# Two transformer layers with a mixture of experts: attention scores from two rounded 32-bit parts, even and odd heads on the two row halves of TensorE

## The reference

```
# layer 0: pre-norm
x = x + attn(ln1(x), ln1(x), causal)          # call 0
x = x + attn(ln2(x), context)                 # call 1
x = x + relu(ln3(x) @ w1 + b1) @ w2 + b2      # FFN, 256 -> 1024 -> 256
# layer 1: post-norm, all norms with gain and shift
x = ln1(x + attn(x, x, causal))               # call 2
x = ln2(x + attn(x, context))                 # call 3
top-2 of 8 experts by softmax(x @ router), shares = softmax of the two weights
x = ln3(x + sum of share * (gelu(x @ e_w1 + e_b1) @ e_w2 + e_b2))
# attn: 16 heads of width 16, softmax(q k^T / 4) v, then an output projection
```

## Time and profile before

| | |
|---|---|
| median of 3 runs | 1273.6 us (1271.52 to 1281.05) |
| the profiled execution | 1274.6 us |
| its span in the trace | 1272.8 us |
| PE busy | 1107.4 us (87%) |
| DVE busy | 836.6 us (66%) |
| ACT busy | 685.6 us (54%) |
| POOL busy | 561.3 us (44%) |

### The profile page before, as it was taken

The page is one execution under the profiler, slowest core; times in us unless marked ns, Lnnn a source line. Parts: engine busy times, 40 slices in busy tenths (PEclk is TensorE's granted clock), DMA queues, the critical chain, the costliest instruction groups (busy, mean ns, idle before and its releaser), DMA issues. The chain is left out here.

```text
span 1272.8 us, 26559 instructions
## 1 busy us (share of the span) xinstructions
PE 1107.4 (87%) x9056; PEld 911.7 (72%) x9056; DVE 836.6 (66%) x1782; ACT 685.6 (54%) x1445; POOL 561.3 (44%) x805
## 2 busy tenths in 40 slices
PE   8789999999999999999999998877289999989840
PEld 7567677778877888877777666544289998989840
DVE  2666667775555444355676777642479999999945
ACT  4355555665555554445566655644176666656522
POOL 4355555322221113345674554433436565656544
PEclk9899999999999999999999989977589999999985
DMA  7666657573333233446575754405477676767663
GB/s 162 99 134 125 95 81 97 85 126 59 51 49 49 39 36 51 84 59 93 119 104 74 106 91 81 77 26 184 148 231 221 195 226 195 236 192 223 208 159 114
DMA packets 106707, 152.20 MB, mean 120 GB/s; under 512 B 19440, under 2 KB 91376, under 8 KB 99824
## 3 DMA queue, kind: packets, MB, share of 16 engines
q1 hardware_dynamic: 98112, 140.09, 50.5%
q0 software_dynamic: 8352, 10.80, 4.4%
q10 hardware_dynamic: 144, 0.02, 0.0%
HBM read 78.39 MB, written 21.62 MB: 79 GB/s over the span
## 5 line engine op out<-in xcount | busy, mean ns | idle before, releaser
L862 ACT ACTIVATE probs<-s 128x384 f32<-128x384 f32 (+1 forms) x512 | 267.8, 541 | 195.2 <-PE s L680 181.8
L932 DVE TENSOR_REDUCE neg_max<-s 128x2 f32<-128x512 f32 x256 | 169.6, 689 | 95.4 <-PE s L657 89.2
L930 DVE TENSOR_REDUCE neg_blocks<-s 128x3 f32<-128x384 f32 x256 | 135.9, 556 | 120.2 <-PE s L654 112.8
L680 PE MATMUL s<-q_stack,k_stack 98*128 98x256 bf16 (+1 forms) x1024 | 175.6, 262 | 14.4 <-ACT probs L862 11.9
L545 POOL TENSOR_SCALAR_AFFINE_SELECT probs<-probs 128x256 f32<-128x256 f32 x256 | 103.1, 411 | 188.1 <-ACT probs L862 187.0
L1284 PE MATMUL moe<-rows_hi,e_w_hi 128*128 128x256 f32 x368 | 106.1, 288 | 25.1 <-DVE rows_lo L1395 25.1
L680 PEld LDWEIGHTS s<-q_stack,k_stack 98*128 98x128 bf16 x1024 | 90.1, 99 | 41.4 <-ACT probs L862 24.4
L699 PE MATMUL pv<-probs,v 128*32 128x256 f32 (+1 forms) x2048 | 115.2, 367 | 2.7 <-POOL probs L545 2.3
L1399 DVE TENSOR_TENSOR e_hidden_lo<-e_hidden,e_hidden_hi 128x512 fp32r<-128x512 f32 x92 | 108.0, 1173 | 10.7 <-ACT e_hidden_hi L1353 10.7
L657 PE MATMUL s<-k_stack,q_stack 96*128 96x256 bf16 x512 | 98.1, 276 | 12.8 <-DVE neg_max L932 11.2
L1284 PE MATMUL moe<-e_w_hi,e_hidden_hi 128*128 128x256 f32 x368 | 104.6, 284 | 1.6 <-DVE e_w_lo L1391 1.6
(11 more groups left out here) (197 smaller groups left out, 2588.9 us busy)
## 6 DMA issues: line engine op xcount, KB each, us to landing
w<-in_expert_w SPq DMA_DIRECT2D x26, 1024.0 KB, 5.4
k_stack<-k_part SPq DMA_DIRECT2D x192, 128.0 KB, 4.1
q_stack<-q_part SPq DMA_DIRECT2D x192, 128.0 KB, 5.8
e_w<-in_expert_w SPq DMA_DIRECT2D x24, 1024.0 KB, 5.3
rows<-slots_x SPq DMA_DIRECT2D x25, 256.0 KB, 2.9
slots_x<-filler SPq DMA_DIRECT2D x8, 518.0 KB, 3.8
cT<-in_context SPq DMA_DIRECT2D x16, 256.0 KB, 4.8
e_b<-in_expert_b SPq DMA_DIRECT2D x24, 128.0 KB, 3.9
```

The source lines that it names most:

```text
L680: last = pe.matmul(dst[:, kt * S:kt * S + S - q0], k[:, kt * P:(kt + 1) * P], q[:, q0:S], start=True, stop=True)
L862: act.activation(probs[hd][:, 0:width], s2[hd % 2][:, 0:width], ACT.Exp, scale=SCALE).then_inc(probs_ready, 1)
L930: dve.tensor_reduce(neg_blocks[:, :, hd], src[:, 0:3 * P].rearrange("p (b s) -> p b s", b=3), AX_X, ALU.max, negate=True).then_inc(s1_free, 1)
L932: dve.tensor_reduce(neg_max[:, :, hd], src[:].rearrange("p (t s) -> p t s", t=TILES), AX_X, ALU.max, negate=True).then_inc(s1_free, 1)
```

## The change

- q and k are split in two parts of `float32r` instead of three of bf16: ACT writes part 0, DVE writes part 1 at once; POOL's two operations go.
- The stacks hold three blocks of 16 rows (products 0 by 0, 0 by 1, 1 by 0) for the even heads from row 0 on and for the odd heads from row 64 on. A score matmul contracts 48 rows (maxima) or 50 rows (scores), starting at row 0 or 64. The copies into the stacks are still six for each of q and k; those of the shift are four instead of two.
- The mask is no longer added on PE. DVE's reduction over a causal head becomes two operations that add the mask and reduce (256 and 128 wide), and the joining copies at the end of a call go.
- ACT fills whole `k_stack` buffers with ones before their first use.
- PE gets transposes without use (`idle_at_end`) before steps of the last lane, and 75 at the end of attention.
- Experts: `second_high` moves from POOL to ACT, behind `rows_high`; b1 comes by a DMA on SP in each step; the gain and shift of the last norm are fetched later.
- Final norm: in place, statistics first, POOL's roots ahead of its gains, and two of eight gains on DVE.
- The plan (`AT`, `PACE`, `LAG`) stays as it is.

The diff, cut to its core:

```diff
-PARTS = 3
-Q_PART_OF_ROWS = (0, 0, 0, 1, 1, 2)
-K_PART_OF_ROWS = (0, 1, 2, 0, 1, 0)
+PARTS = 2
+Q_PART_OF_ROWS = (0, 0, 1)
+K_PART_OF_ROWS = (0, 1, 0)
...
+SIDE = P // KC
...
+WARM_HEAD, WARM_TURN, WARM_OUT_T, WARM_WO, WARM_FINAL_T, WARM_ROUTER, WARM_RANK, WARM_EXPERTS = 2, 5, 11, 7, 34, 5, 12, 75
...
-        STACKED = 16 * len(Q_PART_OF_ROWS)
+        STACKED = 16 * len(Q_PART_OF_ROWS) * KC
+        SHIFTED = 16 * SHIFT_PARTS * KC
+        def head_rows(stack, hd, rows):
+            first = hd % KC * SIDE
+            return stack[first:first + rows, hd // KC, :]
...
-                    if p == i:
-                        sp.dma_start(stack[block * DK:(block + 1) * DK], part[i][:]).then_inc(done, 16)
+                    for side in range(KC):
+                        if p == i:
+                            first = side * SIDE + block * DK
+                            sp.dma_start(stack[first:first + DK].bitcast(F32), part[i][:, side, :].bitcast(F32)).then_inc(done, 16)
...
-                    sp.dma_start(q_stack[buf][PRODUCT_ROWS + i:PRODUCT_ROWS + i + 1], neg_max_T[i][:]).then_inc(shift_stacked[buf], 16)
+                    for side in range(KC):
+                        first = side * SIDE + PRODUCT_ROWS + i
+                        sp.dma_start(q_stack[buf][first:first + 1].bitcast(F32), neg_max_T[i][side * HPC:(side + 1) * HPC, :].bitcast(F32)).then_inc(shift_stacked[buf], 16)
...
-            def split_rest(kind, rest, part, rest_ready, ready):
-                def step(lane, c):
-                    pool.wait_ge(rest_ready, nth(kind, lane, c))
-                    pool.sem_inc(gate, 1)
-                    pool.tensor_copy(part[1][:], rest[:]).then_inc(ready[1], 1)
-                    pool.drain()
-                    pool.tensor_tensor(part[2][:], rest[:], part[1][:], ALU.subtract).then_inc(ready[2], 1)
-                return step
...
-                q, k = q_stack[n % 3][0:PRODUCT_ROWS, hd, :], k_stack[n % 3][0:PRODUCT_ROWS, hd, :]
+                q, k = head_rows(q_stack[n % 3], hd, PRODUCT_ROWS), head_rows(k_stack[n % 3], hd, PRODUCT_ROWS)
...
-                    pe.matmul(dst[:, P:3 * P], ident_b[:], mask_qk[:].rearrange("p b s -> p (b s)"), start=True, stop=False)
-                    pe.matmul(dst[:, 0:S], q[:, P:S], k, start=False, stop=True, skip_group_check=True)
-                    last = pe.matmul(dst[:, S:S + P], q[:, 0:P], k[:, 0:P], start=False, stop=True)
+                    pe.matmul(dst[:, 0:S], q[:, P:S], k, start=True, stop=True)
+                    last = pe.matmul(dst[:, S:S + P], q[:, 0:P], k[:, 0:P], start=True, stop=True)
...
-                    pe.wait_ge(shift_stacked[n % 3], 16 * SHIFT_PARTS * (n // 3 + 1))
-                    if n < len(k_stack):
-                        pe.wait_ge(ones_made, n + 1)
+                    pe.wait_ge(shift_stacked[n % 3], SHIFTED * (n // 3 + 1))
+                if n == NCALL - 1:
+                    idle_at_end(lane, WARM_HEAD)
...
-                q, k = q_stack[n % 3][0:SCORE_ROWS, hd, :], k_stack[n % 3][0:SCORE_ROWS, hd, :]
+                q, k = head_rows(q_stack[n % 3], hd, SCORE_ROWS), head_rows(k_stack[n % 3], hd, SCORE_ROWS)
...
-            def rest(kind, first, dst, bias, first_ready, ready):
+            def rest(kind, part, bias, ready):
...
-                    dve.wait_ge(first_ready, nth(kind, lane, c))
+                    dve.wait_ge(ready[0], nth(kind, lane, c))
-                        dve.scalar_tensor_tensor(out=dst[:, half, :], in0=bank(kind, lane, c)[:, half * S:(half + 1) * S], scalar=bias[c][:, half:half + 1],
-                                                 in1=first[:, half, :], op0=ALU.add, op1=ALU.subtract)
+                        last = dve.scalar_tensor_tensor(out=part[1][:, half, :], in0=bank(kind, lane, c)[:, half * S:(half + 1) * S], scalar=bias[c][:, half:half + 1],
+                                                        in1=part[0][:, half, :].bitcast(F32), op0=ALU.add, op1=ALU.subtract)
+                    last.then_inc(ready[1], 1)
-                    dve.sem_inc(ready, 1)
...
-                src = s1[hd % 2]
+                src, at = s1[hd % 2], hd % KC * HPC + hd // KC
...
-                    dve.tensor_reduce(neg_blocks[:, :, hd], src[:, 0:3 * P].rearrange("p (b s) -> p b s", b=3), AX_X, ALU.max, negate=True).then_inc(s1_free, 1)
+                    dve.tensor_tensor_reduce(src[:, 0:S], src[:, 0:S], mask_qk[:].rearrange("p b s -> p (b s)"), -1.0, -MASKED, ALU.add, ALU.min, neg_max[:, 1, at:at + 1])
+                    dve.tensor_tensor_reduce(src[:, S:S + P], src[:, S:S + P], mask_qk[:, 1, :], -1.0, -MASKED, ALU.add, ALU.min, neg_max[:, 0, at:at + 1]).then_inc(s1_free, 1)
-                    dve.tensor_reduce(neg_max[:, :, hd], src[:].rearrange("p (t s) -> p t s", t=TILES), AX_X, ALU.max, negate=True).then_inc(s1_free, 1)
+                    dve.tensor_reduce(neg_max[:, :, at], src[:].rearrange("p (t s) -> p t s", t=TILES), AX_X, ALU.max, negate=True).then_inc(s1_free, 1)
...
-                    if CAUSAL[c]:
-                        dve.tensor_copy(neg_max[:, 0, :], neg_blocks[:, 2, :])
-                        dve.tensor_tensor(neg_max[:, 1, :], neg_blocks[:, 0, :], neg_blocks[:, 1, :], ALU.min)
-                        dve.drain()
...
-                dve.tensor_tensor(neg_max_T[1][:], bank("shift", lane, c)[0:H, 0:S], neg_max_T[0][:], ALU.subtract).then_inc(shift_T_ready[1], 1)
+                dve.tensor_tensor(neg_max_T[1][:], bank("shift", lane, c)[0:H, 0:S], neg_max_T[0][:].bitcast(F32), ALU.subtract).then_inc(shift_T_ready[1], 1)
...
+            def idle_at_end(lane, turns):
+                if lane == B - 1:
+                    pe.wait_ge(s1_free, NCALL * H)
+                    idle(turns, s1[0])
...
-                act.activation(k_stack[i][PRODUCT_ROWS:SCORE_ROWS].rearrange("p h s -> p (h s)"), ident[PRODUCT_ROWS:SCORE_ROWS, 0:1].to_broadcast([SHIFT_PARTS, H * S]), ACT.Identity, bias=1.0).then_inc(ones_made, 1)
+                act.activation(k_stack[i][:].rearrange("p h s -> p (h s)"), ident[:, 0:1].to_broadcast([P, HPC * S]), ACT.Identity, bias=1.0).then_inc(ones_made, 1)
...
+            def fetch_first_bias(e, i):
+                sp.dma_start(b1_e[i][:].unsqueeze(1), b1[:, bass.ds(e, 1), :]).then_inc(b1_loaded[i], 16)
...
+            fetch_first_bias(0, 0)
+            fetch_first_bias(1, 1)
...
+            fetch_second(1, 1)
-            fetch_second(1, 1)
-            sp.dma_start(gain[:], t["end_gain"].partition_broadcast(P)).then_inc(norm_loaded, 16)
-            sp.dma_start(shift[:], t["end_shift"].partition_broadcast(P)).then_inc(norm_loaded, 16)
...
+                sp.wait_ge(hidden_ready, (n + 1) * QUARTERS)
+                fetch_first_bias(e, i)
...
-                sp.dma_start(out_rows[:, b * TILES:(b + 1) * TILES, :], y[b % 4][:]).then_inc(y_out[b % 4], 16)
-            for i in range(4):
-                sp.wait_ge(y_out[i], 16 * (B // 4))
+                sp.dma_start(out_rows[:, b * TILES:(b + 1) * TILES, :], z[b][:]).then_inc(y_out, 16)
+            sp.wait_ge(norm_loaded, 16 * 2)
+            sp.wait_ge(y_out, 16 * B)
...
-            def second_high(i, nth):
-                pool.wait_ge(w2_loaded[i], 16 * nth)
-                pool.sem_inc(gate, 1)
-                for q in range(QUARTERS):
-                    pool.tensor_copy(w2_hi[i][:, 2 * q:2 * q + 2, :], w2[i][:, 2 * q:2 * q + 2, :]).then_inc(w2_hi_ready, 1)
...
-            for q in range(QUARTERS):
-                pool.tensor_copy(w2_hi[0][:, 2 * q:2 * q + 2, :], w2[0][:, 2 * q:2 * q + 2, :]).then_inc(w2_hi_ready, 1)
...
-                    pool.wait_ge(up_full, n * QUARTERS + 1)
-                    second_high(i, j + 1)
...
-            def gain_of(b):
-                pool.wait_ge(normal_ready, b + 1)
-                pool.tensor_tensor(z[b][:], z[b][:], gain[:].unsqueeze(1).to_broadcast([P, TILES, D]), ALU.mult).then_inc(scaled, 1)
-            for pair in range(B // 2):
+            def inverse_root(pair):
...
-                for b in (2 * pair - 2, 2 * pair - 1):
-                    if b >= 0:
-                        gain_of(b)
-            for b in (B - 2, B - 1):
-                gain_of(b)
+            def gain_of(b):
+                pool.wait_ge(normal_ready, b + 1)
+                pool.tensor_tensor(z[b][:], z[b][:], gain[:].unsqueeze(1).to_broadcast([P, TILES, D]), ALU.mult).then_inc(gained, 1)
+            pool.wait_ge(norm_loaded, 16 * 2)
+            inverse_root(0)
+            inverse_root(1)
+            gain_of(0)
+            inverse_root(2)
+            gain_of(1)
+            gain_of(2)
+            inverse_root(3)
+            for b in range(3, B):
+                if b not in GAIN_BY_DVE:
+                    gain_of(b)
...
+            def second_high(i, nth):
+                if nth is not None:
+                    act.wait_ge(w2_loaded[i], 16 * nth)
+                for q in range(QUARTERS):
```

(42 more changed lines are left out.)

76 lines of the change are left out of this document (28 added, 48 removed).

## The result

The changed kernel takes 1309.3 us (median of 4 runs, 1308.53 to 1313.53), the kernel before 1277.1 (1271.52 to 1281.05): a ratio of 1.026, 95% interval 1.021 to 1.032. The forecast was 1263, and the range ended at 1299. The profiled executions differ by the same amount: spans of 1307.6 and 1272.8, +34.8.

The account below looks back on a forecast made before the run. PE was taken to bound the second call, and the causal calls with slack, DVE second; in the experts PE waited for DVE. Terms summed to -11 us, from 1274.6 profiled to 1263.6, so 1263 against the median; range 1230 to 1299.

Parts of the forecast that it names:

- experts: Expert loop: second_high to ACT and b1 by DMA shorten a tile from 12.91 to 11.75 us; -25 us (-31 to -15).
- final norm: Final norm: statistics first, so DVE no longer waits four rounds for Pool's power and gains; -5 us (0 to -7).
- last lane: Last attention lane: idle transposes fill PE's waits and keep its clock up; -8 us (0 to -9, or +2).
- start: First lanes: Pool's two split operations leave their latency; -2 us (0 to -4), an estimate.
- widths: Score matmuls on PE: 128-wide rounded ones step by 0.112 us, using up the gain from dropping the mask; 0 (-14 if 0.055).
- maxima: Causal row maxima on DVE: two masked reductions add 0.15 us a head, a fifth comes through; +6 us (-3 to +45).
- changes of tiling: Attention on PE: 591 passages between row halves and all rows at 0.09 us, less slack; +36 us (0 to +53).
- overlap of halves: Attention scores on PE: neighbouring steps in different row halves run side by side, about a quarter usable; -13 us (0 to -30).
- Rival 1: Attention scores: tiling changes cost, but halves don't overlap because weight loads queue; 1276 us, chance 0.22.
- Rival 2: Attention scores: changing row halves is free, or the halves are not there; 1227 to 1240 us, say 1238, chance 0.26.
- Rival 3: Causal calls: DVE's masked maxima, at +0.40 us a head, make PE wait; +45 us, 1302 us, chance 0.12.
- three signs of being wrong: Attention gets shorter, PE waits over 20 us for maxima in the causal calls, or the expert period stays over 12.3 us.

Follow-up runs that it names:

- whole array: Changed kernel, but each score matmul contracts rows 0 to 112 (114), summing two heads, and two of four shift copies are left out: 1253.6 us, ratio 0.983.
- old attention: Attention part of the kernel before, joined to the experts and final norm of the changed kernel: 1255.6 us, ratio 0.985.
- one half: Changed kernel, but every head's scores read the lower half of the stacks, so two halves never overlap: 1348.0 us, ratio 1.059.
- bf16 halves: Changed kernel with bf16 parts and stacks in place of the rounded 32-bit ones, same rows and halves: 1274.9 us, ratio 0.997.
- plain maxima: Changed kernel with one plain reduction over three blocks in the causal calls in place of the two masked ones: 1306.4 us.

## Why the prediction was wrong, by its own steps

| term | forecast | found | by |
| --- | --- | --- | --- |
| experts | -25 | -17.0 | the two traces |
| final norm | -5 | -3.6 | the two traces |
| last lane, start, widths, maxima | -8 - 2 + 0 + 6 = -4 | -2.0 together | whole array against old attention |
| changes of tiling | +36 (0 to +53) | +94.4 | one half against whole array |
| overlap of halves | -13 (0 to -30) | -38.7 | one half against changed kernel |
| sum | -11 | +33, measured +32 | |

**The step that failed is "changes of tiling": the price of a passage, and what I took off it for slack.** I took "0.09 each way" from the value matmuls and stopped at the edge: one start to the next. The price has a second part one step further on, 0.10. The kernel before hardly shows it: behind value matmuls come bf16 scores in its order, with a second step of 0.12 for 0.11, and transposes whose weights are 16 columns, 0.115; never a 4-byte load of 128 columns. I carried the price of those over to rounded scores and f32 projections. The earlier trace rows had the bound: such a load is 0.11 long, and a steady row hides it beside the matmul before. At the 0.17 to 0.20 measured, 591 passages are 100 to 118 us, of which 94 came out on the path; with 0.09 my upper bound for the term was 53, and so the range could not hold the result.

The second half of the step was the slack: I counted 16 of 22 us in the causal calls because they "have slack", and 3 of 12 in the last because it "waits for others anyway". The runs showed 39.9 and 17.0 there, 0.13 to 0.18 a passage, against 31.2 in the second call, where 17 were forecast. PE's waits in those calls were too short to take the passages in.

**The overlap** was real and three times the forecast: "PE can use about a quarter" stood against 38.7 of 49 us. Rival 1 (no overlap) is out. It was right about one thing that I had set aside, that a 4-byte load matters; it matters behind edges, not between halves. The net of halves was forecast at +23 and is +55.7.

**The clock** is part of it. In the first causal lanes it was 0.87 after, 0.88 with one half, 0.88 with bf16 halves, 0.90 with plain maxima, and 0.95 to 0.97 in the three kernels whose scores use the whole array; 0.10 of 124.8 us, an upper estimate, would be most of the +13.3 there. Whether the halves themselves or the waits that come with them pull it down is not shown. The second call, at full clock throughout, is free of it, and there the passages, less the overlap, give +19.0. I had no term for the clock in attention.

The rule quoted from the Trainium skill, "TensorEngine Tiling (Array Packing)", section "Tiling Modes", that a change of mode drains TensorE, holds for row halves: 0.09 us at each edge here. It gives no size, and I gave it that of the edge alone; the sum by it, -11, went the wrong way.

**Rival 2** (free passages, or halves that are not there) is out by the runs with the whole array and with one half. **Rival 3** (DVE's maxima bound the causal calls) is out: the two masked operations are 443 and 332 ns against my 0.42 and 0.29, but start to start a head takes 0.60 where they run back to back; PE waited 15.6 us for the maxima of causal heads (2.4 before), under the 20 that I had set, and taking the masks out gave 2.9 us. The 6 us of that term are of the right size, as far as 2.9 us inside the spread can tell.

**Score widths**: 0.11 behind 128-wide rounded scores held (L655 or L681, 0.05 and 0.17 in turn, 0.11 on average). The zero of that term held as far as the 2.0 us of the four terms together can tell.

**Experts**: "SP gets one more issue a tile (about 0.6 us)" was the right place, mis-sized. The b1 issue stands, with two others, a wait and the register reads, ahead of the load that ACT needs next; the tile went at 12.2, where "PE then sets 11.5 us" and 11.75 were forecast. With the load moved it went at 11.63. No run takes the b1 issue out by itself, so its own share stays open. The last subtraction of the halves no longer takes 2.92 us, but neither always 0.68: where Pool's product runs beside it, it takes 1.53, 0.88 on average.

**Idle transposes**: forecast -8, and nothing of it in the total. They hold the clock as the step said, and the stretch behind the last maxima is 4.4 us shorter with them; why the total does not show it stays open.

None of the three signs of being wrong was met: attention got longer, the waits for causal maxima were 15.6 us, the period was 12.2. I had written none for a passage that costs more than its edge.

## What to carry to other kernels

Count how often PE changes between row or column tiles and the whole array in its written order, and charge each change its edge and the step behind the first matmul; with 4-byte operands that was 0.2 us a change, against 0.1 us gained by each pair of short matmuls side by side. I take from it that half-array work pays only in long runs of it; no run here shows one that pays. Nor does a wait elsewhere on the engine pay for the changes: here the calls with slack paid 0.13 to 0.18 us for each, nearly as much as the one without. And where an in-order queue issues many small transfers, put the one that an engine needs soonest ahead of register reads and of those with a tile of slack: that alone was worth 13 us here.

## What I had not expected of the hardware

- A change of row tiling costs 0.09 us, and 0.10 more in the next step where that operand is 4 bytes wide (256-wide matmuls; 0.055 for 128-wide transposes); 0.01 where it is bf16.
- Two rounded matmuls in the two row halves run side by side at full rate: pairs of 256-wide ones step by 0.11 to 0.12, as a single one of the whole array does.
- The granted clock was lower where scores use half the rows: 0.87 to 0.90 against 0.95 to 0.97 in the same lanes; what of it is the halves and what is PE's waits was not kept apart.
- A masked maximum on DVE leaves two records, 443 ns of work on 256 columns and 142 ns of reading the accumulator; the second begins with the next operation and hides beside it.
